# Copies of the second attention's keys all on VectorE, setup loads on SyncE's queue, and other slots for two units and the last group

## What is computed

```python
# first layer: 20 heads of 64
n = layer_norm(x, ln1);  x = x + attention(n, n,       a1_wq, a1_wk, a1_wv, a1_wo, a1_bo)
n = layer_norm(x, ln2);  x = x + attention(n, context, a2_wq, a2_wk, a2_wv, a2_wo, a2_bo)
x = geglu_ff(layer_norm(x, ln3)) + x
# second layer: 20 heads of 8; 73 text tokens and 4 image tokens of the context
q = heads(x @ W_q); k_t = heads(text @ W_k); v_t = heads(text @ W_v)
probs_t = softmax(q @ k_t.T * scale);  text_out = probs_t @ v_t
sem = l2norm(probs_t @ text) @ l2norm(ip).T
probs_ip = softmax(q @ k_ip.T * scale + 0.5 * sem) * mask
out = (text_out + probs_ip @ v_ip) @ W_out + b_out + x
```

## Time and profile before

| | us |
|---|---|
| median of 3 runs | 3834.04 |
| lowest, highest | 3832.09, 3839.49 |
| the profiled execution's own time | 3831.53 |
| its span, first to last instruction | 3829.7 |

### The profile page before, as it was taken

The page is one execution under the profiler, slowest core; times in us unless marked ns, Lnnn a source line. Parts: engine busy times, 40 slices in busy tenths (PEclk is TensorE's granted clock), DMA queues, the critical chain, the costliest instruction groups (busy, mean ns, idle before and its releaser), DMA issues. The chain is left out here.

```text
span 3829.7 us, 88852 instructions
## 1 busy us (share of the span) xinstructions
PE 3622.5 (95%) x29632; PEld 3341.0 (87%) x29632; DVE 2563.7 (67%) x8159; ACT 2584.0 (67%) x8021; POOL 1335.9 (35%) x1658
## 2 busy tenths in 40 slices
PE   5999999999999999999999999999999999999988
PEld 5888989889898898989989898898988989899877
DVE  6667676676766767676676766767667676766755
ACT  5666676766767667676676767667676676766654
POOL 2233343333433334343333433334333343433323
PEclk9999999999999999999999999999999999999986
DMA  5522313223141322313223142231323223132220
GB/s 160 168 65 75 101 46 118 60 86 89 45 121 55 97 78 59 113 47 108 66 77 99 46 121 56 86 89 45 120 56 96 78 58 114 48 108 64 76 67 12
DMA packets 210716, 313.38 MB, mean 82 GB/s; under 512 B 31232, under 2 KB 167520, under 8 KB 210272
## 3 DMA queue, kind: packets, MB, share of 16 engines
q1 hardware_dynamic: 207392, 306.87, 27.2%
q10 hardware_dynamic: 2880, 0.83, 0.1%
HBM read 267.97 MB, written 14.42 MB: 74 GB/s over the span
## 5 line engine op out<-in xcount | busy, mean ns | idle before, releaser
L1376 POOL TENSOR_TENSOR SE<-SE,rs 128x512 f32<-128x512 f32 (+1 forms) x640 | 556.5, 870 | 1792.2 <-DVE rs L1210 1792.2
L961 ACT ACTIVATE SE<-PS,mx 128x128 f32<-128x128 f32 (+2 forms) x3840 | 979.0, 345 | 255.1 <-DVE qq L1234 109.1
L816 PE MATMUL PT<-ident,SE 128*128 128x128 f32 (+2 forms) x3840 | 585.9, 276 | 36.2 <-POOL SE L1376 35.3
L947 ACT ACTIVATE PTs<-PT 128x512 f32<-128x512 f32 (+2 forms) x960 | 574.7, 599 | 58.1 <-PE PT L816 38.7
L1205 DVE TENSOR_REDUCE sums<-SE 128x4 f32<-128x512 f32 (+1 forms) x640 | 366.8, 573 | 341.1 <-ACT SE L961 338.8
L1194 DVE TENSOR_REDUCE mx<-PS 128x4 f32<-128x512 f32 (+2 forms) x960 | 505.0, 526 | 59.4 <-PE PS L794 42.3
L816 PEld LDWEIGHTS PT<-ident,SE 128*128 128x128 f32 (+2 forms) x3840 | 469.9, 145 | 63.7 <-POOL SE L1376 49.6
L1368 POOL TENSOR_TENSOR n<-qq,p_half 128x4 f32<-128x4 f32 x320 | 323.0, 1009 | 469.1 <-DVE qq L1234 469.0
L774 PE MATMUL PW<-w_o,OTs 128*128 128x160 f32 x2560 | 417.0, 300 | 1.0 <-ACT OTs L939 1.0
L794 PE MATMUL PS<-qk 128*128 128x256 f32 x1280 | 348.9, 395 | 47.5 <-ACT qk L887 47.5
L884 ACT ACTIVATE qk<-PG 128x256 f32<-128x256 f32 x640 | 252.2, 394 | 196.1 <-PE PG L620 192.2
(11 more groups left out here) (205 smaller groups left out, 7853.5 us busy)
## 6 DMA issues: line engine op xcount, KB each, us to landing
q_slice<-q_split SPq DMA_DIRECT2D x630, 192.0 KB, 2.5
vc_slice<-vc_split SPq DMA_DIRECT2D x155, 512.0 KB, 3.6
kc_slice<-kc_split SPq DMA_DIRECT2D x150, 256.0 KB, 2.7
q1st<-q_hi SPq DMA_DIRECT2D x320, 32.0 KB, 1.9
k1st<-k_hi SPq DMA_DIRECT2D x160, 38.5 KB, 1.9
xres<-in_x_dram SPq DMA_DIRECT2D x32, 160.0 KB, 2.3
q1st<-q_lo SPq DMA_DIRECT2D x160, 32.0 KB, 1.9
out_dram<-x SPq DMA_DIRECT2D x64, 80.0 KB, 1.6
```

The costliest lines, as they stand in the source:

```text
L816: last = tr(PT[0:J, 128 * i:128 * i + 128], SE[:, place % 4, J * i:J * i + J], ident[:, :])
L947: a_(PTs[0:J, place % 3, :], PT[0:J, :], ACT.Copy).then_inc(S["pts_done"], 1)
L961: last = a_(SE[:, place % 4, J * i:J * i + J], PS[place % 2][:, step * i:step * i + J], ACT.Exp, bias=mx[:, place % 2, i:i + 1])
L1376: gp.tensor_tensor(e, e, rs[:, n % 2, :].unsqueeze(2).to_broadcast([128, 4, J]), ALU.mult)\
```

## The change

**Copies of kc.** ScalarE's two copies of each kc job go; VectorE makes all four, signals `kc_done` after the first two and `kc_dve` after the last two, and waits for the job alone.

**Slots.** Two second-layer units of every group move from slots 37 and 41 to 36 and 38, and the first layer's units around them move by one. The split of w_k_rem moves from slot 9 to 16. K1 for the first 128 columns moves from 52 to 53. In the last group the normalisations (2,1), (3,0) and (3,1) move from 65, 60, 71 to 63, 58, 69, the second feed-forward half from 68 to 67, Q1 from 62 and 73 to 61 and 72, and ctx1 of its four batches from 58, 65, 80, 85 to 59, 64, 80, 84.

**Loads.** The five loads of w_v leave the setup block and stand first in SyncE's part of the main block. Of `EARLY`, ScalarE keeps the first two; the other ten are issued by SyncE at slot 10.

```diff
-    L1_SLOT = [6, 7, 9, 10, 11, 13, 14, 15, 17, 18, 22, 26, 27, 29, 33, 37, 41, 45, 49, 53]
+    L1_SLOT = [6, 7, 9, 10, 11, 13, 14, 15, 17, 18, 22, 26, 27, 29, 33, 36, 38, 45, 49, 53]
...
-    SPLIT_SLOT = [8, 9, 17, 18, 28, 30, 31, 31, 32, 32, 49, 50]
+    SPLIT_SLOT = [8, 16, 17, 18, 28, 30, 31, 31, 32, 32, 49, 50]
...
+    EARLY_SLOT = 10
...
-    K1_SLOT = (52, 58)
+    K1_SLOT = (53, 58)
...
-    LAST_CTX1_SLOT = {0: 58, 1: 65, 2: 80, 3: 85}
+    LAST_NORM_SLOT = {(2, 0): 52, (2, 1): 63, (3, 0): 58, (3, 1): 69}
+    LAST_FF_SLOT = [56, 56, 56, 56, 56, 67, 67, 67, 67, 67]
+    LAST_Q1_SLOT = [61, 72]
+    LAST_CTX1_SLOT = {0: 59, 1: 64, 2: 80, 3: 84}
...
-                for i in range(2, 4):
-                    for src, p0, p1 in SPLITS[i][0]:
-                        sp.dma_start(SPLITS[i][3][p0:p1], src).then_inc(split_in[i], 16)
...
-                for i, (dst, src) in enumerate(EARLY):
-                    act.dma_start(dst, src, allow_slow_non_contiguous=True).then_inc(ln_in if i < 2 else early_in, 16)
+                for dst, src in EARLY[0:2]:
+                    act.dma_start(dst, src, allow_slow_non_contiguous=True).then_inc(ln_in, 16)
...
+                for i in range(2, 4):
+                    for src, p0, p1 in SPLITS[i][0]:
+                        sp.dma_start(SPLITS[i][3][p0:p1], src).then_inc(split_in[i], 16)
                 for t in range(FIRST, LAST):
+                    if t == EARLY_SLOT:
+                        for dst, src in EARLY[2:]:
+                            sp.dma_start(dst, src, allow_slow_non_contiguous=True).then_inc(early_in, 16)
...
-                    elif kind == "kc":
-                        ps = take(name)
-                        for e in range(2):
-                            rows = slice(DH * e, DH * e + DH)
-                            last = a_(kx[0][rows, i % 2, e, :].rearrange("p (b t) -> p b t", t=T),
-                                      ps[rows, 0:HB * TS].rearrange("p (b t) -> p b t", t=TS)[:, :, 0:T], ACT.Copy)
-                        last.then_inc(S["kc_done"], 1)
...
-                        dve.wait_ge(S["kc_done"], NP * g + i + 1)
-                        for e in range(2):
-                            rows = slice(DH * e, DH * e + DH)
-                            last = v.tensor_copy(kx[1][rows, i, e, :].rearrange("p (b t) -> p b t", t=T),
-                                                 ps[rows, HB * TS:2 * HB * TS].rearrange("p (b t) -> p b t", t=TS)[:, :, 0:T])
-                        last.then_inc(S["kc_dve"], 1)
+                        for h in range(2):
+                            for e in range(2):
+                                rows = slice(DH * e, DH * e + DH)
+                                last = v.tensor_copy(kx[h][rows, i if h else i % 2, e, :].rearrange("p (b t) -> p b t", t=T),
+                                                     ps[rows, HB * TS * h:HB * TS * h + HB * TS]
+                                                     .rearrange("p (b t) -> p b t", t=TS)[:, :, 0:T])
+                            last.then_inc(S["kc_dve" if h else "kc_done"], 1)
```

More of the change, by code:

```diff
@@ L43, in xattn_program @@
     STEP = 60
-    L1_SLOT = [6, 7, 9, 10, 11, 13, 14, 15, 17, 18, 22, 26, 27, 29, 33, 37, 41, 45, 49, 53]
-    LAST_L1_SLOT = list(range(4, 14)) + list(range(20, 30))
+    L1_SLOT = [6, 7, 9, 10, 11, 13, 14, 15, 17, 18, 22, 26, 27, 29, 33, 36, 38, 45, 49, 53]
+    LAST_L1_SLOT = [4, 5, 6, 7, 8, 9, 10, 11, 12, 13, 20, 21, 22, 23, 24, 25, 26, 27, 28, 29]
     L0_SLOT = [s for s in range(STEP) if s not in L1_SLOT]
@@ L372, in xattn_program, with norm_slot, ff_slot, q1_slot @@
         outputs_at = slots((product_slot(UNIT_AT[t]) + OUT_LAG - PV_LAG, UNIT_AT[t]) for t in sorted(UNIT_AT))
-        NORMS = sorted((STEP * g + (s if g else FIRST_NORM_SLOT.get((k, h), s)), g, k, h)
-                       for g in range(GROUPS) for (k, h), s in NORM_SLOT.items())
+        def norm_slot(g, k, h):
+            own = FIRST_NORM_SLOT if g == 0 else LAST_NORM_SLOT if g == GROUPS - 1 else {}
+            return STEP * g + own.get((k, h), NORM_SLOT[(k, h)])
+        def ff_slot(g):
+            return FF_SLOT if g < GROUPS - 1 else LAST_FF_SLOT
+        def q1_slot(g):
+            return Q1_SLOT if g < GROUPS - 1 else LAST_Q1_SLOT
+        NORMS = sorted((norm_slot(g, k, h), g, k, h) for g in range(GROUPS) for k, h in NORM_SLOT)
         NORM = {x[1:]: i for i, x in enumerate(NORMS)}
@@ L390, in ctx1_slot @@
             return STEP * g + (CTX1_SLOT if g < GROUPS - 1 else LAST_CTX1_SLOT)[b]
-        stacks_at = slots([(STEP * g + Q1_SLOT[h] + 1 + w, ("q1", g, h, w))
+        stacks_at = slots([(STEP * g + q1_slot(g)[h] + 1 + w, ("q1", g, h, w))
                            for g in range(GROUPS) for h in range(2) for w in range(W1)]
@@ L398, in xattn_program @@
             + [(t + (1 if k == 3 else 2), ("xT", g, k, h)) for t, g, k, h in NORMS]
-            + [(STEP * g + Q1_SLOT[h], ("q1", g, h)) for g in range(GROUPS) for h in range(2)]
+            + [(STEP * g + q1_slot(g)[h], ("q1", g, h)) for g in range(GROUPS) for h in range(2)]
             + [(STEP * g + PREP_SLOT[h] + 1, ("cT", g, h)) for g in range(GROUPS) for h in range(2)]
@@ L402, in xattn_program @@
                for g in range(GROUPS) for b in range(GB)]
-            + [(STEP * g + FF_SLOT[F * h + F - 1] + 1, ("down", g, h)) for g in range(GROUPS) for h in range(2)]
-            + [(STEP * g + s, ("ff", g, i)) for g in range(GROUPS) for i, s in enumerate(FF_SLOT)]
+            + [(STEP * g + ff_slot(g)[F * h + F - 1] + 1, ("down", g, h)) for g in range(GROUPS) for h in range(2)]
+            + [(STEP * g + s, ("ff", g, i)) for g in range(GROUPS) for i, s in enumerate(ff_slot(g))]
             + [(STEP * g + K1_SLOT[r], ("k1", g, r)) for g in range(GROUPS) for r in range(2)]
```

## The result

The changed kernel takes 3841.7 us (median of 20 runs, 3836.85 to 3852.58); the kernel before, run beside it, 3832.36 (median of 20, 3825.39 to 3839.49). The ratio is 1.0029, 95% interval 1.0021 to 1.0036: the change makes the kernel 8 to 14 us **slower** (11 by the ratio, 9.3 by the two medians). The forecast was 3829, a little faster.

The account below looks back on a forecast made before the run. Neither VectorE nor ScalarE bounds the whole; their work costs time only where TensorE (223.45 of 232 us busy) waits. Start -8.5, group 0 +2, groups +14.4, end -11.5 sum to -3.6 against 3831.53: 3827.9, raised to 3829; range 3811 to 3848.

Parts of the forecast that it names:

- 0.65 + 0.7 + 0.5: kc stretch, us per group: wait before slot 37's scores, wait at slot 42's scores, and 0.17 + 0.3 behind it.
- the -0.9: kc stretch: today's TensorE waits of 0.56 and two of some 0.2 us go when units 37 and 41 move.
- The start, -8.5: Setup: loads leave the block, so TensorE's first job starts at 21.8 us in place of 30.32.
- The bound of -6: Start: smaller gain of 6 us if weights land 2.5 us later because all loads share the same engines as before.
- Rival E: Start: setup issue time moves with the loads, fside's 9.45 us holds SyncE before the stores; only -2, 3835.5 us; chance .08.
- Group 0, +2: Group 0's kc stretch: an extra pair of VectorE copies (0.64 us) shows in about three of ten jobs; range 0 to +4.
- The last group, -11.5: Last group's open chain: earlier normalisation and q1, later ctx1 of batch 0; first score -8.5 us, -11.5 down to the second FF.
- D: Last group: the end gives nothing, because SyncE's six stack issues of about 0.6 us lie between scores; 3840.5 us; chance .07.
- F: Last group: it keeps the full clock, a quarter of 27.5 busy us back, -7; 3822 us; chance .07.
- C: kc stretch: VectorE becomes the bound, copies show in slots 37, 39, 41 and 43; 2.3 us a group, 3849; chance .16.
- a sum of 12.1 against 12.2: kc stretch, slots 39 to 41 up to slot 41's first pair: VectorE's queue 12.1 us, TensorE's load 12.2 us, called equal.
- B: kc stretch: copies are hidden by two jobs of slack and 4.4 us free on VectorE; groups +0.1, about 3815 us; chance .24.

Follow-up runs that it names:

- the six without the tables: Six profiled kernels lacking the last group's new slots, among them the kernel before and the setup part alone; slot 44 of group 15 to the end took 175.5 to 183.2 us.
- the kernel that shares two jobs: Changed kernel, but ScalarE again makes the first pair of copies in the kc jobs of units 22 and 26; median 3812.78 us, ratio 0.9953 to the kernel before.

## Why the prediction was wrong

Its sum was -8.5 + 2 + 14.4 - 11.5 = -3.6; the two profiles show -5.6 + 7.1 + 29.8 - 13.5 = +17.8, of which 7.5 belong to the profiled execution and not to the median. By the runs of the parts, the costs were forecast well and the gains were not: the kc copies at 15 x 1.85 + 2 = 29.8 us, measured 32; what was set against them at 13.5 + 8.5 + 11.5 = 33.5, measured 21. Each part alone, the last group gave 6.9 for 11.5, the start 4.2 for 8.5, the moved units 3.4 for 13.5, and K1, which was not priced, 8.4, each to some 3.5 us either way. That turned the sign.

- **The kc stretch, the failed step.** The new costs were forecast at 0.65 + 0.7 + 0.5 = 1.85 a group; measured 1.69, at the two places named. What failed is the -0.9 set against them, the 0.56 and the "two of some 0.2" that were to go. In the kc stretch of group 5 in the kernel before, TensorE's matmuls have the wait of 0.56 and no other of 0.2 or more. It did go, but with the units in their new places two others came, of 0.26 and 0.20, so the step was worth 0.13 a group. K1, which was not priced, gave 0.28. So the net is +1.24 and not +0.96 (the terms as written add up to 0.95), 18.6 us and not 14.4.
- **The clock in the groups, not seen.** The other 11 us of the +29.8 are almost all eight more falls of the clock at slot 32, nine against one, 1.3 each (10.4). The kernel before has the waits in front of them in every group all the same. The prediction read the granted clock of a middle group as 1.00 and put their price at nothing, without a row for the other groups. The profiled execution is 7.5 us above its median and has a lower mean clock (0.986) than fourteen of the twenty. At 1.3 us a fall the median execution would have some six falls fewer, so three of the nine, and 4 us (an estimate; one profile of each kernel does not show it).
- **The start, -8.5 for -5.6.** The step that failed is "issued from 5.54, they take 10.2 us to land, so until about 15.7". It adds the median of four loads to the start of the first issue; the copy waits for the last of them, which already in the kernel before landed at 18.6 and now lands at 19.3. The bound of -6 was drawn for late weights: the first product gained 6.2, the first softmax 5.6. Rival E was wrong in its price, as the start gained more than 2, and fside was issued in 1.93. But a hold like the one it feared was there on another load: the x load held SyncE for 8.34 us before the stores. Whether w_k_rem stands before or behind moved the first product by 3.3 us and the first softmax by 0.1, in the kernel without the kc part. In the medians the part is worth -4.2.
- **Group 0, +2 for +7.1.** The copies are 1.2 of it (0.54 and 0.70 at slots 39 and 43). Most of the rest comes in slots 49 to 54, with longer waits for a q slice (3.49 for 2.45) and two longer falls of the clock. Slots 49 to 59 are 4 to 5 us longer than before in four of the eight profiles with the new K1 slot, 0.5 to 2.1 longer in the other four, and at most 0.6 longer without it; no run asked why. Over all profiles the start of group 1 lies between 222.0 and 229.1 us with the setup part and between 227.5 and 236.9 without: group 0 scatters by more than the term, and one profile does not price it.
- **The last group, -11.5 for -13.5** in the profile. The mechanism held: of the 8.5 to the first score 4.6 were to come behind the PT, and it is 6.0 there, a part of it because the q1 matmuls now run at full clock. In the medians it is -6.9. The profile of the kernel before has one of the longest ends among the six without the tables (175.5 to 183.2), so -13.5 is at the upper side; the rest stays open. D (nothing from the end) was wrong. F asked for the full clock: it was 0.69 in that stretch, for 0.50.
- **Rivals.** C (+2.3 a group, VectorE the bound of the stretch, 3849) named the right side at .16. Its four places were two: only the copies ahead of the scores of units 22 and 26 cost. The row that spoke for it stood in the prediction: slot 39 with 5.05 us of VectorE's work against 3.9, and a sum of 12.1 against 12.2. Where the two queues were equally long, what was added showed; it was priced, and then balanced with a gain from the order that no row showed to be free. B failed at those two jobs; the copies of the other eight cost 3 us of the 32.
- **The Trainium skill's cost of the copy** (VectorE: DVE Perf Modes, errata section) would have made the pair 0.57; four copies took 1.31, 0.66 a pair, so the row was the better price. The Trainium skill's advice that offloading a saturated VectorE to ScalarE may make sense (Perfetto Trace Analysis, Optimizing Scalar/DVE Operations) agrees with the kernel that shares two jobs, 29 us faster, if saturation is read between two handovers and not on the mean of 69%.

Three kernels beat both: the change without its kc part, 3810.4 us, the same with w_k_rem at slot 9, 3812.5, and the change with two jobs shared, 3812.8. Their intervals against the kernel before overlap.

## What to carry to other kernels

A busy share of 68%, and even 29.4 of 33.85 us in a stretch, says nothing on whether 0.64 us more will show: add up the queue between two handovers, and where the two engines' sums are equal, expect a wait. Here eight of ten additions cost next to nothing and two cost 29 us. A wait that a new order removes is a gain only if none takes its place: look for what the new order puts ahead of the next handover. When several loads share a semaphore, count from the last one's issue. When a bundle of edits is judged, undo the suspect alone before anything else: here one part cost 32 us and hid 21 that the others gave. Price every number that moves; the one left out was worth 4 us in the groups and perhaps 8 in all.

## What the runs showed of the hardware

Waits of 0.84 and 0.70 us within two slots, in the same code, were followed by a fall of the granted clock to 0.65 on the mean of 4.5 us in some groups and not in others; each fall cost 1.3 us. Nine such falls are 12 us, and the fastest and the slowest of twenty executions of the program are 16 us apart, with mean granted clocks of 0.989 and 0.984. So the spread goes with the clock; that it is these falls is likely and was not shown, as only one execution has a trace.

A DMA issue can hold its engine long after others of its size: one x load was in issue for 8.34 us on SyncE, where five weight loads before it took 2.21 together; before the change it was fside on ScalarE with 9.45, where fside later took 1.93 on SyncE. In both cases the load stood behind the bulk of the weights, and the hold ended 0.5 to 0.6 us after the last q weight load had landed (19.2 for 18.6 before, 19.8 for 19.3 after). What held the issue is not shown.
